# Expert stages: logits of all groups added into one bank, statistics two groups ahead, lists in tile pairs, scatters ahead of later gathers

## The chip, the cores and the metric

The kernel runs as one launch on one core of one Trainium2 chip. The metric is the device time in microseconds. Of the kernel before there are three timed runs and one profiled execution. The core has a matrix engine (PE, with its weight loads as PEld), a vector engine (DVE), an activation engine (ACT), a general engine (POOL) that also issues gathers and scatters by index, and SP, which issues plain transfers.

## What is computed

Three layers follow each other on x, 8192 tokens of 256 numbers in fp32: a mixture of experts, attention, and the same mixture of experts again.

```python
x = x + 0.5 * ffn(layernorm(x))
x = x + attn(layernorm(x))
x = x + 0.5 * ffn(layernorm(x))
```

Only the two ffn layers matter here. Their routing, cut to its core:

```python
probs = softmax(xf @ gate_w.T)            # 8192 tokens, 8 experts
order = argsort(-probs)                   # experts of a token, likeliest first
# a token chooses experts until their probabilities reach 0.9
# an expert keeps 1024 tokens at most: those with the highest p - rank
scores = where(chosen & kept, probs, 0)
h = gelu(xf @ w1[e].T); y = h @ w2[e].T   # for each expert e
out = sum over e of scores[:, e] * y
```

## The kernel before

build_ffn is called for each ffn layer (names "ffn1" and "ffn2", shown as ffn). Token p * 64 + t lies on partition p, tile t. An expert stage has these parts.

- **Front.** 16 groups of 4 tiles. SP loads a group into one of four buffers xin (L232). DVE takes mean and variance (statistics, L420 to L427), ACT the root (L351), DVE the reciprocal and the shift (scale, L434 and L435), ACT normalises four tiles (normalise, L356), PE turns the group (turn, L611), ACT copies it out (turn, L364), and PE multiplies it with the gate (logits, L620): 8 rows of 512 logits in one of two banks. DVE copies these into logitT (take_logits, L440). SP writes the normalised rows of groups 0 to 7 to the DRAM table at once, those of 8 to 15 after the last logits (L235).
- **Hand-over.** Eight transfers bring logitT (one expert a partition) into prob (one token block a partition), four from SP and four from ACT (L247, L376). DVE takes the maximum and subtracts it, ACT takes the exponential, DVE compares the experts with each other and PE sums (L469 to L482, L634, L636).
- **Search.** 27 steps of halving find each expert's threshold (L506 to L512, L640).
- **Lists.** For expert e, DVE builds 0/1 matrices that say which slot each token goes to (picks and finish_picks, L558 to L565, in the memory of logitT). PE multiplies them tile by tile, 64 matmuls (slots, L657). DVE takes the list of tokens (take_idx, L545), SP moves it to idx_all (L265).
- **Expert loop.** POOL gathers 1024 rows of the table in 8 instructions (gather, L316). PE turns weights and rows, multiplies with w1 and w2 (L673 to L705), ACT copies and takes Gelu, DVE scales each of 8 tiles of y by slot_score (L573, L578), and POOL adds them to the output in DRAM (scatter, L326).

Each engine works through its own list in order, so what waits holds back all behind it. gather(e) waits until the rows of e - 2 are turned, its slot_score is taken and list e is there; scatter(e) waits for all of y of e and for the landing of scatter(e - 1). POOL's order is written out:

```python
for e in range(NE):
    if e + 2 < NE:
        gather(e + 2)
    scatter(e)
```

PE's order is slots(0), slots(1), then expert(e), slots(e + 2). DVE's is picks(e + 2), finish_picks(e + 2), expert(e), take_idx(e + 2).

## Time and profile before

| | us |
|---|---|
| median of three runs | 3117.75 (3116.11 to 3124.43) |
| profiled execution, its own time | 3118.9 |
| its span | 3117.1 |
| expert stages | 431 and 431 |
| attention | 2255 |

| engine | busy us | share |
|---|---|---|
| PE | 2613.3 | 84% |
| PEld | 2049.8 | 66% |
| DVE | 1689.6 | 54% |
| ACT | 1684.7 | 54% |
| POOL | 537.1 | 17% |

The profile is one execution. Its times run from the start of the span. Shares are means over stages with different limits, so each stage is read by itself: in the timeline a row has its start, its duration, the engine, the line and operation, what it writes from what, how often, and in brackets how long its engine stood idle before it and what ended that. The granted clock is a share of TensorE's full 2.4 GHz; at 0.5 it is 1.2 GHz.

### The profile page before, as it was taken

What the parts mean: (1) busy time and instruction counts of PE and PEld (TensorE: products, weight loads), DVE (VectorE), ACT (ScalarE), POOL (GpSimd) and SP (SyncE); (2) the same over time, 40 slices, a digit from 0 to 9 for tenths busy, and PEclk for the clock granted to TensorE, in tenths of its full rate; (3) what the DMA queues carried; (4) which work ended last, traced back from release to release, by engine and by line L of the source; (5) the groups of instructions that cost most, each with busy time, mean ns of one, the idle gap of its engine ahead of it and who ended that gap; (6) DMA issues with size and microseconds to landing.
All of it is one profiled execution on the core that took longest, in us unless ns stands there. A gap on an engine that the chain in (4) does not pass through costs nothing. (4 is left out here: it accounts for less than half of the span.)

```text
span 3117.1 us, 106343 instructions
## 1 busy us (share of the span) xinstructions
PE 2613.3 (84%) x48002; PEld 2049.8 (66%) x48004; DVE 1689.6 (54%) x3557; ACT 1684.7 (54%) x2130; POOL 537.1 (17%) x527
## 2 busy tenths in 40 slices
PE   6369924554999999999999999999999999562995
PEld 2157712223888888888888788888898888322674
DVE  5543218887667666665766576656322222356331
ACT  5112203334777777777777777777666666330221
POOL 1028740000100000010001000000000000100586
PEclk8668966666999999999999999999999999885887
DMA  5615531001111111112111211121111111541465
GB/s 162 178 43 101 95 51 31 27 28 48 39 56 49 39 56 45 55 44 67 52 52 49 62 53 52 44 67 43 56 41 47 41 47 34 155 115 26 87 103 67
DMA packets 172434, 195.31 MB, mean 63 GB/s; under 512 B 35600, under 2 KB 151328, under 8 KB 171808
## 3 DMA queue, kind: packets, MB, share of 16 engines
q1 hardware_dynamic: 145056, 153.27, 16.6%
q0 software_dynamic: 24576, 34.10, 7.0%
q8 instruction: 407, 6.67, 0.9%
q10 hardware_dynamic: 2304, 0.53, 0.2%
q14 instruction: 91, 0.75, 0.1%
HBM read 119.10 MB, written 76.02 MB: 63 GB/s over the span
## 5 line engine op out<-in xcount | busy, mean ns | idle before, releaser
L1090 ACT ACTIVATE at_ew<-at_ring 128x1024 f32<-128x1024 f32 (+2 forms) x1280 | 1116.8, 899 | 402.6 <-PE at_ring L1465 287.5
L1488 PEld LDWEIGHTS at_mix<-at_val,at_ew 128*64 128x64 f32 x34816 | 1212.5, 137 | 155.1 <-issue 20.7
L1488 PE MATMUL at_mix<-at_val,at_ew 128*64 128x68 f32 x34816 | 1259.2, 223 | 4.5 <-issue 3.9
L1465 PE MATMUL at_ring<-at_qT,at_kT 98*64 98x512 bf16 (+3 forms) x5120 | 732.9, 350 | 17.4 <-DMA at_kT<-k_parts 11.6
L1337 DVE TENSOR_TENSOR at_mixed<-at_mix,at_prob 128x272 f32<-128x272 f32 x256 | 112.5, 439 | 572.9 <-PE at_mix L1488 556.2
L1465 PEld LDWEIGHTS at_ring<-at_qT,at_kT 98*64 98x64 bf16 x5120 | 268.0, 111 | 81.5 <-issue 26.4
L1035 POOL TENSOR_TENSOR at_val<-at_prob,at_eps_t 128x64 f32<-128x64 f32 x64 | 19.5, 305 | 1228.2 <-PE at_mix L1488 1228.2
L391 ACT ACTIVATE ffn_w1T<-ffn_pair 128x512 f32<-128x512 f32 x16 | 9.6, 597 | 394.8 <-PE ffn_pair L677 394.8
L1540 PE MATMUL at_side<-at_w_all,at_turned 128*64 128x512 f32 (+1 forms) x1024 | 208.4, 554 | 14.8 <-ACT at_vo L1110 7.8
L326 POOL DMA_INDIRECT out_dram<-ffn_xn,ffn_idx_all x128 | 207.9, 1624 | 47.8 <-issue 37.5
L1469 PE MATMUL at_ring<-at_late_kq,at_ident_b 128*64 128x128 bf16 x2048 | 205.6, 220 | 0.0
L316 POOL DMA_INDIRECT ffn_xn<-table,ffn_idx_all x128 | 128.5, 1004 | 442.5 <-DMA ffn_idx_all<-ffn_idx_hi 384.3
L1340 DVE TENSOR_REDUCE at_summed<-at_mixed 128x68 f32<-128x272 f32 x256 | 160.5, 627 | 8.8
L1540 PEld LDWEIGHTS at_side<-at_w_all,at_turned 128*64 128x64 f32 x1024 | 73.2, 149 | 115.1 <-issue 72.4
L1278 DVE TENSOR_REDUCE at_sums<-at_prods 128x1024 f32<-128x4096 f32 x32 | 141.3, 4416 | 0.3
L657 PE MATMUL ffn_bank<-ffn_logitT 128*32 128x64 bf16 x1024 | 119.0, 290 | 22.5 <-DVE ffn_logitT L565 22.5
L578 DVE TENSOR_SCALAR ffn_xn<-ffn_bank,ffn_slot_score 128x256 f32<-128x256 f32 x128 | 61.7, 484 | 138.7 <-PE ffn_bank L705 138.6
L657 PEld LDWEIGHTS ffn_bank<-ffn_logitT 128*32 128x32 bf16 x1024 | 114.8, 137 | 27.2 <-DVE ffn_logitT L565 23.2
L1038 POOL TENSOR_TENSOR at_val<-at_vo,at_val 128x1024 f32<-128x1024 f32 x64 | 130.0, 2032 | 5.0
L1469 PEld LDWEIGHTS at_ring<-at_late_kq,at_ident_b 128*64 128x64 bf16 x2048 | 124.5, 111 | 2.8 <-issue 0.3
L1051 POOL TENSOR_TENSOR at_acc<-at_acc,at_prob 128x64 f32<-128x64 f32 x28 | 8.9, 319 | 664.8 <-PE at_side L1587 664.8
L705 PE MATMUL ffn_bank<-ffn_w2T,ffn_xn 128*128 128x256 f32 x512 | 116.6, 384 | 3.1 <-DVE ffn_xn L578 3.1
(222 smaller groups left out, 3016.3 us busy)
## 6 DMA issues: line engine op xcount, KB each, us to landing
table<-ffn_xn SPq DMA_DIRECT2D x32, 512.0 KB, 6.1
q_parts<-at_parts SPq DMA_DIRECT2D x64, 192.0 KB, 2.4
k_parts<-at_parts SPq DMA_DIRECT2D x64, 192.0 KB, 2.8
at_qT<-q_parts SPq DMA_DIRECT2D x64, 192.0 KB
at_kT<-k_parts SPq DMA_DIRECT2D x64, 192.0 KB
ffn_xin<-in_L_attn_x_dram SPq DMA_DIRECT2D x16, 512.0 KB, 4.2
ffn_w_in<-in_L_ffn_w_dram SPq DMA_DIRECT2D x32, 256.0 KB, 3.3
at_xin<-out_dram SPq DMA_DIRECT2D x32, 256.0 KB, 3.4
```

Of the source, the lines that this page charges most:

```text
L316: pool.indirect_dma_start(out=rows[e % 2][:, j, :], out_offset=None, in_=table, in_offset=bass.IndirectOffsetOnAxis(ap=idx_all[:, e * J + ...
L326: pool.indirect_dma_start(out=dst, out_offset=bass.IndirectOffsetOnAxis(ap=idx_all[:, e * J + j:e * J + j + 1], axis=0), in_=y[e % 2][:, j ...
L657: last = pe.matmul(idx_ps_bank[0:SLOT_HI, 0:2 * SLOT_LO], pick_hi[q][:, :, t], pick_lo[q][:, :, t], start=(t == 0), stop=(t == T - 1))
L705: last = pe.matmul(bank[2 + j % 2][:, 0:D], hT[:, f, j * P:(j + 1) * P], w2T[q][:, f, :], start=(f == 0), stop=(f == FK - 1))
L1038: pool.tensor_tensor(val[q][:, :, :, 0:HD], vv.unsqueeze(2).to_broadcast([P, TB, K, HD]), val[q][:, :, :, HD].unsqueeze(3).to_broadcast([P ...
L1090: act.activation(ew[u % NE_BUF][:, 0:w], ring[u % 2][:, 0:w], ACT.Exp).then_inc(s["exp_ready"], 1)
L1278: ch(dve.tensor_reduce(sums[:, :, :].rearrange("p c n -> p (c n)"), prods[:, :, :].rearrange("p c (n k) -> p (c n) k", k=K), AX.X, ALU.add))
L1340: ch(dve.tensor_reduce(summed[:, :, :], mixed[:, :, :, :].rearrange("p t k w -> p t w k"), AX.X, ALU.add))
L1465: lastm = pe.matmul(ring[u % 2][h:h + HALF, at:at + w], kT[q][:, (j + n) * P + h:(j + n) * P + h + HALF], qT[q][:, c * 512 + t * P:(c + 1) ...
L1469: lastm = pe.matmul(ring[u % 2][h:h + HALF, at:at + P], ident_b[:, h:h + HALF], late_kq[:, :], start=False, stop=True)
L1488: lastm = pe.matmul(mix[c % 2][h:h + HALF, t * K * VW:(t + 1) * K * VW], ew[u % NE_BUF][:, col + h:col + h + HALF], val[q][:, j + n, :, :] ...
L1540: lastm = pe.matmul(side[h:h + HALF, g * 512:g * 512 + n], turned[0][:, g * DK + k, h:h + HALF], w_all[:, k, first:first + n], start=(k == ...
```

## The change

It touches build_ffn alone, in seven places.

1. The gate lies in gateZ, 8 columns of weights between two blocks of 120 columns of zeros. For group g a window of 128 columns is taken so that the 8 gate columns write rows 8g to 8g + 7. All 32 logit matmuls add into bank[0]. ACT copies the bank once, PE turns it in four pieces into bank[1], and DVE reads it there. The 16 copies and the 8 transfers of logits go.
2. DVE runs the statistics two groups ahead of scale (three sets of buffers), with six xin buffers. It normalises the first of four tiles itself, ACT the other three.
3. SP stores groups 0 to 5 in the front and 6 to 15 after the last group.
4. digits, pick_hi and pick_lo keep two tiles beside each other: index (t // 2, digit, t % 2) in place of (digit, t).
5. POOL scatters e before it gathers e + 2, and waits for each tile of y by itself.
6. DVE takes slot_score of e before it builds list e + 2, and waits for the landing of scatter(e - 2) only after that.
7. ACT loads the table of Gelu during routing.

```diff
-    XB = 4
-    EARLY = G // 2
+    XB = 6
+    SB = 3
+    EARLY = 6
+    ZW = P - NE
...
-        gateT = sb("gateT", [P, DK, NE])
-
-        xin = [sb(f"xin{b}", [P, GT, D]) for b in range(XB)]
+        gateZ = sb("gateZ", [P, DK, ZW + NE + ZW])
+
+        front = sb("front", [P, XB * GT * D + 2 * DK * GT * P])
...
+        def pairs(tile, at, n):
+            return tile[:, at:at + n].bitcast(BF16).rearrange("p (t d i) -> p t d i", t=T // 2, i=2)
+
+        PK = SLOT_LO * T // 2
+        pick_hi = [pairs(front, 3 * q * PK, PK) for q in range(2)]
+        pick_lo = [pairs(front, 3 * q * PK + PK, 2 * PK) for q in range(2)]
+        pick_p = [a[:, :, 0:SLOT_LO, :] for a in pick_lo]
+        pick_t = [a[:, :, SLOT_LO:, :] for a in pick_lo]
...
-                    sp.wait_ge(xn_ready, g + 1)
+                    sp.wait_ge(xn_act, g + 1)
+                    sp.wait_ge(xn_dve, g + 1)
                     if g + XB < G:
                         load(g + XB)
                     if g < EARLY:
                         store(g)
-                sp.wait_ge(logits_ready, G)
-                for e in range(1, NE, 2):
-                    sp.dma_start(prob[:, e, :], logitT[e:e + 1, :].rearrange("e (p t) -> e p t", t=T)).then_inc(logits_moved, 16)
                 for g in range(EARLY, G):
                     store(g)
                 sp.wait_ge(order_ready, 1)
...
                 def scatter(e):
                     if e >= 1:
                         pool.wait_ge(added, e * J * 16)
-                    pool.wait_ge(y_ready, e * J + J)
                     for j in range(J):
+                        pool.wait_ge(y_ready, e * J + j + 1)
...
                 for e in range(NE):
+                    scatter(e)
                     if e + 2 < NE:
                         gather(e + 2)
-                    scatter(e)
...
-                act.wait_ge(logits_ready, G)
-                for e in range(0, NE, 2):
-                    act.dma_start(prob[:, e, :], logitT[e:e + 1, :].rearrange("e (p t) -> e p t", t=T)).then_inc(logits_moved, 16)
+                act.wait_ge(logits_ps, G)
+                act.activation(logitG[:, :], bank[0][:, :], ACT.Copy).then_inc(logits_ready, 1)
...
+                    if g >= SB:
+                        dve.wait_ge(xn_act, g - SB + 1)
...
-                dve.wait_ge(consts_ready, 2)
+                    dve.tensor_scalar(xnG[g][:, 0, :], xin[g % XB][:, 0, :], mv[q][:, 0, 0:1], rstd[q][:, 0:1],
+                                      ALU.subtract, ALU.mult).then_inc(xn_dve, 1)
+
+                for g in range(2):
+                    statistics(g)
                 for g in range(G):
-                    if g + 1 < G:
-                        statistics(g + 1)
+                    if g + 2 < G:
+                        statistics(g + 2)
                     scale(g)
-                    if g >= 2:
-                        take_logits(g - 2)
-                take_logits(G - 2)
-                take_logits(G - 1)
...
-                dve.wait_ge(logits_moved, MOVES)
-                ch(dve.tensor_reduce(row_t[:, :], by_t(prob), AX.X, ALU.max))
-                dve.tensor_tensor(work[:, :, :], prob[:, :, :], over_e(row_t[:, :]), ALU.subtract).then_inc(shifted, 1)
+                row_g = row_t[:, :].rearrange("p (g t) -> p g t", t=GT)
+                logit = bank[1][:, :].rearrange("p (t g e) -> p t g e", t=GT, g=G)
+                dve.wait_ge(turns_ps, G + 2)
+                ch(dve.tensor_reduce(row_g, logit.rearrange("p t g e -> p g t e"), AX.X, ALU.max))
+                dve.tensor_tensor(work[:, :, :].rearrange("p e (g t) -> p e g t", t=GT),
+                                  logit.rearrange("p t g e -> p e g t"),
+                                  row_g.unsqueeze(1).to_broadcast([P, NE, G, GT]), ALU.subtract).then_inc(shifted, 1)
...
+                shape = [P, T // 2, SLOT_LO, 2]
...
                     def of(a):
-                        return a[:, e, :].unsqueeze(1).to_broadcast(shape)
-
-                    ch.add(dve.tensor_tensor(pick_hi[q], digits[:, :, :], of(hi), ALU.is_equal))
-                    ch(dve.tensor_tensor(pick_lo[q][:, 0:SLOT_LO, :], digits[:, :, :], of(lo), ALU.is_equal))
-                    ch(dve.tensor_tensor(pick_lo[q][:, SLOT_LO:, :], pick_lo[q][:, 0:SLOT_LO, :],
-                                         count_b[:, :].unsqueeze(1).to_broadcast(shape), ALU.mult))
+                        return a.rearrange("p (t i) -> p t i", i=2).unsqueeze(2).to_broadcast(shape)
+
+                    digit = digits[:, :, :].unsqueeze(1).to_broadcast(shape)
+                    ch.add(dve.tensor_tensor(pick_hi[q], digit, of(hi[:, e, :]), ALU.is_equal))
+                    ch(dve.tensor_tensor(pick_p[q], digit, of(lo[:, e, :]), ALU.is_equal))
+                    ch(dve.tensor_tensor(pick_t[q], pick_p[q], of(count_b[:, :]), ALU.mult))
 
                 def finish_picks(e):
                     q = e % 2
-                    dve.tensor_scalar(pick_lo[q][:, 0:SLOT_LO, :], pick_lo[q][:, 0:SLOT_LO, :], part[:, 0:1], None,
-                                      ALU.mult).then_inc(picks_ready, 1)
+                    dve.tensor_scalar(pick_p[q], pick_p[q], part[:, 0:1], None, ALU.mult).then_inc(picks_ready, 1)
 
                 def expert(e):
                     q = e % 2
                     dve.wait_ge(gathered[q], (e // 2 + 1) * 16 * J)
+                    dve.tensor_scalar(slot_score[q][:, :], rows[q][:, :, D + e], 0.5, None, ALU.mult
+                                      ).then_inc(slot_score_ready, 1)
+                    if e + 2 < NE:
+                        picks(e + 2)
+                        finish_picks(e + 2)
+                    dve.wait_ge(slot_score_ready, e + 1)
                     if e >= 2:
                         dve.wait_ge(added, (e - 1) * J * 16)
-                    dve.tensor_scalar(slot_score[q][:, :], rows[q][:, :, D + e], 0.5, None, ALU.mult
-                                      ).then_inc(slot_score_ready, 1)
-                    dve.wait_ge(slot_score_ready, e + 1)
...
                 def logits(g):
                     pe.wait_ge(xnT_ready, g + 1)
-                    if g >= 2:
-                        pe.wait_ge(logits_ready, g - 1)
+                    at = ZW - g * NE
                     for k in range(DK):
-                        last = pe.matmul(bank[g % 2][0:NE, :], gateT[:, k, :], xnT[g % 2][:, k, :],
-                                         start=(k == 0), stop=(k == DK - 1))
+                        last = pe.matmul(bank[0][:, :], gateZ[:, k, at:at + P], xnT[g % 2][:, k, :],
+                                         start=(g == 0 and k == 0), stop=(g == G - 1 and k == DK - 1))
                     last.then_inc(logits_ps, 1)
 
...
                 logits(G - 1)
+                pe.wait_ge(logits_ready, 1)
+                for t in range(GT):
+                    last = pe.transpose(bank[1][:, t * P:(t + 1) * P], logitG[:, t * P:(t + 1) * P], ident[:, :])
+                last.then_inc(turns_ps, 1)
...
-                        last = pe.matmul(idx_ps_bank[0:SLOT_HI, 0:2 * SLOT_LO], pick_hi[q][:, :, t], pick_lo[q][:, :, t],
-                                         start=(t == 0), stop=(t == T - 1))
+                        last = pe.matmul(idx_ps_bank[0:SLOT_HI, 0:2 * SLOT_LO], pick_hi[q][:, t // 2, :, t % 2],
+                                         pick_lo[q][:, t // 2, :, t % 2], start=(t == 0), stop=(t == T - 1))
```

POOL, from its last constants to the end of the expert stage (L316 and L318 gather, L326 and L328 scatter). Before:

```order
L305 MEMSET ffn_restart 128x8
L306 COPY ffn_digits<-ffn_count_b 128x2048
L316 DMA ffn_xn<-table,ffn_idx_all 128x264 x24
L326 DMA out_dram<-ffn_xn,ffn_idx_all 8192x256 x8
L316 DMA ffn_xn<-table,ffn_idx_all 128x264 x8
...
L326 DMA out_dram<-ffn_xn,ffn_idx_all 8192x256 x24
```

The same place in the changed kernel:

```order
L307 MEMSET ffn_restart 128x8
L308 COPY ffn_digits<-ffn_count_b 128x64
L318 DMA ffn_xn<-table,ffn_idx_all 128x264 x16
L328 DMA out_dram<-ffn_xn,ffn_idx_all 8192x256 x8
L318 DMA ffn_xn<-table,ffn_idx_all 128x264 x8
...
L328 DMA out_dram<-ffn_xn,ffn_idx_all 8192x256 x16
```

Two batches of gathers and not three stand ahead of the first scatters, and two batches of scatters and not three are left at the end.

DVE, one group in the steady front (ffn_mv and ffn_var are mean and variance). Before:

```order
L435 SCALAR_TENSOR_TENSOR ffn_shift<-ffn_mv,ffn_rstd 128x4
L440 COPY ffn_logitT<-ffn_bank 8x4x128
L420 BN_STATS ffn_stats<-ffn_xin 128x6 x4
L423 BN_AGGR ffn_mv<-ffn_stats 128x2 x4
L427 TENSOR_SCALAR ffn_var<-ffn_mv 128x4
L434 RECIPROCAL ffn_rstd<-ffn_std 128x4
```

The same place in the changed kernel (ffn_front holds xin):

```order
L434 SCALAR_TENSOR_TENSOR ffn_shift<-ffn_mv,ffn_rstd 128x4
L436 TENSOR_SCALAR ffn_xn<-ffn_front,ffn_mv,ffn_rstd 128x256
L421 BN_STATS ffn_stats<-ffn_front 128x6 x4
L426 BN_AGGR ffn_mv<-ffn_stats 128x2 x4
L428 TENSOR_SCALAR ffn_var<-ffn_mv 128x4
L433 RECIPROCAL ffn_rstd<-ffn_std 128x4
```

The copy that waits for PE's logits is gone; a normalisation of one tile, which waits for nothing of PE, stands there.

## Rows read from the trace of the kernel before

**Rows 1.** busy us by stage: PE, PEld, DVE, ACT, POOL; then clock, DMA share, GB/s

```profile
0.00:431.00 431.00, 281.07 (x1337) 189.41 (x1338) 176.23 (x498) 100.18 (x167) 177.99 (x151) 0.78 0.50 110
...
2686.00:3117.00 431.00, 282.93 (x1337) 190.03 (x1338) 176.27 (x498) 98.89 (x166) 177.62 (x147) 0.75 0.44 91
```

**Rows 2.** the timeline, steady front: start, us, engine, line, operation, [idle before, its end]

```profile
52.07 1.10 PE L611 MATMUL ffn_pair<-ffn_ident,ffn_xn 128*128 128x128 f32 x8
...
52.18 1.04 DVE L440 COPY ffn_logitT<-ffn_bank 8x512 f32<-8x512 f32 x1 [3.70 <-PE ffn_bank L620]
...
53.10 1.88 PE L620 MATMUL ffn_bank<-ffn_xnT,ffn_gateT 128*8 128x512 f32 x4
...
55.38 2.07 ACT L356 ACTIVATE ffn_xn<-ffn_xin,ffn_shift,ffn_rstd 128x256 f32<-128x256 f32 x4
...
57.36 1.00 ACT L364 ACTIVATE ffn_xnT<-ffn_pair 128x1024 f32<-128x1024 f32 x1
...
57.50 1.09 PE L611 MATMUL ffn_pair<-ffn_ident,ffn_xn 128*128 128x128 f32 x8 [2.52 <-ACT ffn_xn L356]
...
62.01 1.09 PE L611 MATMUL ffn_pair<-ffn_ident,ffn_xn 128*128 128x128 f32 x8
```

**Rows 3.** the table of busy time, a stretch of the front, one around the second list

```profile
16.00:50.00 34.00, 26.02 (x90) 11.63 (x91) 20.27 (x84) 23.36 (x48) 0.00 (x0) 0.87 0.74 222
...
182.00:205.00 23.00, 16.18 (x133) 15.33 (x131) 8.48 (x12) 1.09 (x2) 10.28 (x9) 0.50 0.25 71
```

**Rows 4.** the timeline, start of the front

```profile
13.90 1.40 DVE L420 BATCH_NORM_STATS2 ffn_stats<-ffn_xin 128x6 f32<-128x256 f32 x4
...
16.11 1.40 DVE L420 BATCH_NORM_STATS2 ffn_stats<-ffn_xin 128x6 f32<-128x256 f32 x4
...
16.24 1.94 PE L611 MATMUL ffn_pair<-ffn_ident,ffn_xn 128*128 128x128 f32 x8 [13.33 <-ACT ffn_xn L356]
```

**Rows 5.** the timeline, from the front to routing

```profile
95.41 13.05 SPq L235 DMA_DIRECT2D table<-ffn_xn  x8
...
101.99 1.01 DVE L459 TENSOR_REDUCE ffn_row_t<-ffn_prob 128x64 f32<-128x512 f32 x1 [12.81 <-DMA ffn_prob<-ffn_logitT]
...
121.58 2.58 SPq L252 DMA_DIRECT2D ffn_key<-ffn_order  x4
```

**Rows 6.** the timeline, end of the search, first list, first gather

```profile
171.09 0.19 PE L644 MATMUL ffn_bank<-ffn_total,ffn_before 128*128 128x8 bf16 x1 [3.96 <-DVE ffn_total L522]
...
171.19 0.17 PE L647 MATMUL ffn_bank<-ffn_total,ffn_ones 128*128 128x8 bf16 x1
...
181.42 7.43 PE L657 MATMUL ffn_bank<-ffn_logitT 128*32 128x64 bf16 x64 [10.06 <-DVE ffn_logitT L565]
...
183.67 1.23 DVE L560 TENSOR_TENSOR ffn_logitT<-ffn_logitT,ffn_count_b 128x2048 bf16<-128x2048 bf16 x1
...
192.14 1.19 POOL L316 DMA_INDIRECT ffn_xn<-table,ffn_idx_all  x1 [180.48 <-DMA ffn_idx_all<-ffn_idx_hi]
```

**Rows 7.** the timeline, expert loop: DVE, POOL and PE

```profile
216.84 0.48 DVE L578 TENSOR_SCALAR ffn_xn<-ffn_bank,ffn_slot_score 128x256 f32<-128x256 f32 x1 [11.19 <-PE ffn_bank L705]
...
233.35 1.86 POOL L316 DMA_INDIRECT ffn_xn<-table,ffn_idx_all  x1 [19.75 <-PE ffn_pair L685]
...
248.66 7.44 PE L657 MATMUL ffn_bank<-ffn_logitT 128*32 128x64 bf16 x64
...
257.40 2.82 POOL L326 DMA_INDIRECT out_dram<-ffn_xn,ffn_idx_all  x1 [0.31 <-issue]
...
275.00 7.43 PE L657 MATMUL ffn_bank<-ffn_logitT 128*32 128x64 bf16 x64
...
365.70 1.02 POOL L316 DMA_INDIRECT ffn_xn<-table,ffn_idx_all  x1 [1.65 <-DMA ffn_idx_all<-ffn_idx_hi]
...
410.00 1.55 POOL L326 DMA_INDIRECT out_dram<-ffn_xn,ffn_idx_all  x1 [2.53 <-DMA out_dram<-ffn_xn,ffn_idx_all]
...
423.00 1.55 POOL L326 DMA_INDIRECT out_dram<-ffn_xn,ffn_idx_all  x1 [0.30 <-issue]
```

More of the change, by code:

```diff
@@ L97, in build_ffn @@
         gate_in = sb("gate_in", [NE, D])
[L98 to L100 removed]
+        gateZ = sb("gateZ", [P, DK, ZW + NE + ZW])
+        front = sb("front", [P, XB * GT * D + 2 * DK * GT * P])
         xn = sb("xn", [P, T * D])
[L102 to L109 removed]
+        stats = [sb(f"stats{q}", [P, GT, 6]) for q in range(SB)]
+        mv = [sb(f"mv{q}", [P, GT, 2]) for q in range(SB)]
+        var = [sb(f"var{q}", [P, GT]) for q in range(SB)]
+        std = [sb(f"std{q}", [P, GT]) for q in range(SB)]
+        rstd = [sb(f"rstd{q}", [P, GT]) for q in range(SB)]
+        shift = [sb(f"shift{q}", [P, GT]) for q in range(SB)]
+        logitG = sb("logitG", [P, GT * P])
         prob = sb("prob", [P, NE, T])
@@ L132, in build_ffn, with words @@
         lo = sb("lo", [P, NE, T], mybir.dt.int16)
-        def words(tile, at, n, shape, dt=F32):
-            flat = tile[:, at:at + n]
-            if dt != F32:
-                flat = flat.bitcast(dt)
-            return flat.rearrange("p (a b) -> p a b", a=shape[0])
-        PH, PL = SLOT_LO * T // 2, SLOT_LO * T
-        pick_hi = [words(logitT, q * PH, PH, (SLOT_LO, T), BF16) for q in range(2)]
-        pick_lo = [words(logitT, 2 * PH + q * PL, PL, (2 * SLOT_LO, T), BF16) for q in range(2)]
-        xnG = [words(xn, g * GT * D, GT * D, (GT, D)) for g in range(G)]
-        rows = [words(xn, q * J * ROW, J * ROW, (J, ROW)) for q in range(2)]
+        def words(tile, at, n, rows):
+            return tile[:, at:at + n].rearrange("p (a b) -> p a b", a=rows)
+        def pairs(tile, at, n):
[5 more added lines that the diff above has]
+        pick_t = [a[:, :, SLOT_LO:, :] for a in pick_lo]
+        xin = [words(front, b * GT * D, GT * D, GT) for b in range(XB)]
+        xnT = [words(front, XB * GT * D + q * DK * GT * P, DK * GT * P, DK) for q in range(2)]
+        xnG = [words(xn, g * GT * D, GT * D, GT) for g in range(G)]
+        rows = [words(xn, q * J * ROW, J * ROW, J) for q in range(2)]
         used = 2 * J * ROW
-        y = [words(xn, used + q * J * D, J * D, (J, D)) for q in range(2)]
+        y = [words(xn, used + q * J * D, J * D, J) for q in range(2)]
         used += 2 * J * D
-        xeT = words(xn, used, DK * CAP, (DK, CAP))
-        hT = words(xn, used + DK * CAP, FK * CAP, (FK, CAP))
+        xeT = words(xn, used, DK * CAP, DK)
+        hT = words(xn, used + DK * CAP, FK * CAP, FK)
         tile_of = sb("tile_of", [SLOT_HI, SLOT_LO])
@@ L344, in _ @@
             def _(act):
[L345 to L346 removed]
+                act.wait_ge(turns_ps, 1)
+                act.activation(gateZ[:, :, ZW:ZW + NE], bank[1][:, 0:DK * NE].rearrange("p (k e) -> p k e", k=DK),
                                ACT.Copy).then_inc(gateT_ready, 1)
@@ L350, in root @@
                     act.wait_ge(var_ready, g + 1)
-                    act.activation(std[g % 2][:, :], var[g % 2][:, :], ACT.Sqrt).then_inc(std_ready, 1)
+                    act.activation(std[g % SB][:, :], var[g % SB][:, :], ACT.Sqrt).then_inc(std_ready, 1)
                 def normalise(g):
                     act.wait_ge(rstd_ready, g + 1)
-                    for t in range(GT):
+                    for t in range(1, GT):
                         last = act.activation(xnG[g][:, t, :], xin[g % XB][:, t, :], ACT.Identity,
-                                              bias=shift[g % 2][:, t:t + 1], scale=rstd[g % 2][:, t:t + 1])
-                    last.then_inc(xn_ready, 1)
+                                              bias=shift[g % SB][:, t:t + 1], scale=rstd[g % SB][:, t:t + 1])
+                    last.then_inc(xn_act, 1)
                 def turn(g):
-                    act.wait_ge(xnT_ps, g + 1)
+                    act.wait_ge(turns_ps, g + 2)
                     if g >= 2:
                         act.wait_ge(logits_ps, g - 1)
-                    act.activation(xnT[g % 2][:, :, :], pair[g % 2][:, :, :], ACT.Copy).then_inc(xnT_ready, 1)
+                    act.activation(xnT[g % 2], pair[g % 2][:, :, :], ACT.Copy).then_inc(xnT_ready, 1)
                 root(0)
@@ L379, in _ @@
                 act.activation(prob[:, :, :], work[:, :, :], ACT.Exp).then_inc(exped, 1)
+                act.activation(std[1][:, :], var[1][:, :], ACT.Gelu)
                 act.wait_ge(order_ready, 1)
```

61 lines of the change are left out of this document (19 added, 42 removed).

## The prediction, made before the changed kernel ran

> **What bounds the kernel now.** I read the busy time by stage first. It cuts the run into an expert stage of 431 us, attention, and a second expert stage of 431 us whose counts and busy times are those of the first within 2 us [rows 1]. The change touches the expert stages alone, so I work out one, with its times, and take it twice. Attention (2686 - 431 = 2255 us) stays.
>
> In an expert stage four stretches follow each other: the front (layer norm and logits, 16 groups), the hand-over to routing, the search and lists, and the expert loop. The timeline of each shows which wait ends last.
>
> *Front.* Two turns of PE, the second ones of two pairs of groups, start at 52.07 and 62.01: 9.94 us for two groups, 4.97 each. The reader is to see a ring in it. DVE stands 3.70 us before a copy of logits because the copy of group g-2 is queued ahead of the statistics of the next group; so ACT gets its variance late, and PE its rows 2.52 us late [rows 2]. No engine is full. PE is busy 26.02 of 34 us, at a mean granted clock of 0.87: it changes between 2.4 GHz, where a turn takes 1.10 us, and 1.2 GHz, where one takes 1.94 [rows 2 to 4].
>
> *Hand-over.* From the last logits to the first reduction DVE waits 12.81 us for transfers of logitT to prob [rows 5].
>
> *Search and lists.* The 27 search steps are not touched. Then 64 small matmuls per expert list take 7.43 us, 116 ns a pair of weight load and matmul [rows 6].
>
> *Loop.* Two engines are full here. PE repeats every 26.3 us (248.66 to 275.00). POOL repeats every 26.2 us: gathers begin at 233.35 and, five batches later, at 365.70, less 1.35 of an idle 1.65. Of it 8 scatters at 1.86 (1.55 and 0.30 idle, as at 423.00) are 14.9, and some 1.3 are lost where DVE builds a list (the scatter at 257.40 takes 2.82 and not 1.55); that leaves 10.0 for 8 gathers. But POOL stood idle 19.75 us before 233.35, although outputs of expert 0 were there from 217.3 on: gather(2) was in front of scatter(0). At the other end three batches of scatters are left. The last begins at 410.00, 2.53 us after the one before, whose landing it waits for, and its last instruction starts at 423.00 [rows 7].
>
> **The change part by part, one expert stage.**
>
> *Front: logits added in one bank, statistics two ahead, one normalisation of four on DVE.* The logit copies and their waits go; the ring is open. Next late is the fullest engine. PE: a turn 1.03 (52.07 to 53.10) and logits 1.88, 2.9 us a group; the gate now has 128 columns, the rows streamed are still 512, so I add nothing. ACT: three normalisations of 0.52, a turn of 1.00 and a root of 0.2, 2.75. DVE: 2.21 a group now (13.90 to 16.11) and at most 0.48 more for 256 elements, the price of L578, 2.7 [rows 2, 4, 7]. The hand-offs fit: ACT's turn of g-1 runs beside PE's turn of g. One wait is new: DVE's aggregates for g+2 wait until ACT has normalised g-1, and scale(g) is queued behind them. From there to the shift are 0.8 us of DVE work (2.21 less 1.40), during which ACT has its turn of 1.00 to do; it costs ACT some 0.1. So 2.9 us a group at 2.4 GHz. From below 2.7 (DVE or ACT); from above 4.97 as today.
>
> The start gains nothing: POOL's constants hold DVE as now, and three groups of statistics come before the first scale. PE starts at 15.8 (16.24 less one normalisation) and at the low clock, a turn 1.94. With two low turns and one set of logits the third turn starts at 22.6 (estimate). Thirteen groups later, at 60.3, comes turn 15; then 1.05 of turn, twice 1.85 of logits, 0.65 for ACT's copy of the bank (512 elements, an estimate from 1.00 for 1024), 0.6 for four transposes, 0.1: the reduction starts at 66.4 where it started at 101.99. **Saved: 35.6 us**, of which 12.8 is the transfer wait. The reduction and subtraction now read PSUM with strides: between -0.4 and +0.5 us, taken as 0.
>
> The stores: ten and not eight follow the last group. They were issued in 13.05 us for eight, 1.63 each; 16.3 us from 60.2 to 76.5, landed by about 82. The keys are moved at 66.4 + 19.6 = 86 (121.58 - 101.99 = 19.6) [rows 5]. So they keep clear, by some 4 us; if not, the keys wait for the difference. The Gelu table load moves beside DVE's compares; it stood beside running matmuls, so 0.
>
> *Lists in tile pairs.* Before, neighbouring elements of an operand of the list matmuls lay 64 elements (128 bytes) apart, now 2 (4 bytes). At 190 us the granted clock is 0.50, in the loop it is mostly high, and lists take 7.43 or 7.44 us in both [rows 3, 6, 7], so what limits is not the array's clock. Nearest row without a stride: the four matmuls of 8 columns with 128-column weights, the first of which starts at 171.09 and the last at 171.19, 33 ns apart. So a list costs between 64 x 33 ns = 2.1 and 7.4 us. I take 3.9 at the high clock and 4.5 at the low one, nearer the row without stride but with 64 columns to stream. The Trainium skill (SBUF - State Buffer, the note on cachelines) has SBUF lines of 16 bytes, full rate with two or more hits a line, and a penalty on each new line: 8 bf16 may be strided for free. By that rule the old lists pay on every element and the new ones nothing; the trace's equal time at two clocks agrees with it, and it would put the lists at the low end, which saves at most 1 us more a stage.
>
> The first list is followed by DVE's second one, which ends at 184.90 (183.67 + 1.23), before take_idx; so at most 4.0 us are won. **Saved before the first gather: 2.9 us** (0 to 4.0).
>
> *Scatters ahead of later gathers; DVE takes slot_score before the next list.* Time from the first gather on (192.14 before). Gather 0 is free of DVE's list 2, which now waits for it: landed at 12.0 (13.3 before); the first output comes 11.8 us after landing (DVE stood 11.19 between its slot_score and that output [rows 7], and the two take 0.65). So scatter 0 starts at 24.0, in what was idle. Then seven batches of scatters and six of gathers follow without a gap, 26.2 a pair: scatter 6 starts at 24.0 + 157.2 = 181.2, ends at 196.1, scatter 7 waits 2.5 us for that landing, as the batch at 410.00, starts at 198.6; its last instruction at 211.6. Before: 423.00 - 192.14 = 230.9. What is behind the new wait: gather(e+2) stands behind scatter(e), which waits for y of e; PE has expert e+1 to do meanwhile. PE needs 26.3 - 3.5 = 22.8 a period, so it has 3.4 us to spare, and y of 7 is there some 4 us before scatter 7. POOL is the only bound. **Saved: 19 us**, 18.6 with a hand-off (from 0 if PE starves to 20).
>
> **Sum.** 35.6 + 2.9 + 18.6 = 57.1 us a stage, 114.2 in two. The profiled execution took 3118.9 us (span 3117.1), 1.15 above the median of the three runs, 3117.75. 3118.9 - 114.2 = 3004.7, **forecast 3005 us** (its own range 2990 to 3018: 2.7 us a group gives 6 less, 3.1 six more, the rest from lists and hand-offs).
>
> **Rivals.**
> 1. *The clock stays at 1.2 GHz in the front.* For it: the mean is 0.87 now, and the start is low [rows 3, 4]. Against: the fall follows gaps of 2.5 us and more, which go. A group takes 1.94 + 3.5 = 5.4 us (twice 1.88 is 3.8, less what overlaps); the reduction comes at about 107, 5 us later than now. A stage still saves 16: 3087. Chance 0.05.
> 2. *The new list layout halves DVE's rate.* Three of the four list operations take 1.23 for 2048 bf16 elements; with one operand in runs of two they could take 2.4. Then the first index comes 3.2 us later and not 2.9 earlier, and POOL loses one more us at each of six lists: 13 us a stage, 3030. The Trainium skill (VectorE: DVE Perf Modes, what auto-detection checks) asks of 16-bit operands only a step of one innermost, which the pair layout keeps; that speaks against this rival. Chance 0.08.
> 3. *List matmuls do not get faster.* Then PE's period stays 26.3, its first output of expert 7 comes at 24 + 7 x 26.3 = 208.1, 9.5 us behind 198.6, and the 2.9 are lost: 12.4 us a stage, 3030. Against: equal time at two clocks. Chance 0.09.
> 4. *The reordering brings nothing*, since gathers come late and PE starves: 3005 + 37 = 3042. Against: PE's spare time above. Chance 0.04.
> 5. *Slower: list matmuls get slower*, because both operands now hit the same lines of memory. A list of L us gives PE a period of 18.9 + L; scatter 7 then ends at 24 + 7 (18.9 + L) + 14.9 = 171.2 + 7L after the first gather, against 232.8 now, and the first gather comes L - 7.4 later. The 35.6 us of the front are eaten where 8L - 69 exceeds them, from L = 13.1, 204 ns a pair against 116. At 256 ns, L = 16.4, a stage is 26.6 us longer: 3172. No row speaks for it. Chance 0.02.
>
> **How the numbers follow.** The forecast has 0.71, the rivals 0.28, and 0.01 is left for sums that cancel. The range reaches from the forecast's low end to rivals 2, 3 and partly 4: 2988 to 3040. A measurement tells 0.3%, some 9 us, from no change. Faster 0.97, same 0.01, slower 0.02.
>
> **What would show it.** Front: PE turns about 2.9 us apart with the clock at 1.0; no DVE wait before a logit copy; the reduction near 66. If ACT or DVE is full and PE waits, the 2.9 was wrong. Lists: L657's successor under 4 us. Loop: a scatter batch near 24 us after the first gather, 26.2 us per pair on POOL, no idle time over 0.5 us but before scatter 7; PE waiting for gathers. A first expert stage longer than 380 us would make the forecast wrong.

## The result, and the profile after

The changed kernel takes 3007.3 us (median of 4 runs, 3003.83 to 3009.3) beside 3118.22 us of the kernel before on the same chip (3116.11 to 3124.43): ratio 0.964, interval 0.9623 to 0.9657. The forecast was 3005. The profiled execution took 3003.83 us, its span is 3002.0.

The windows of the two expert stages, with the columns of [rows 1], and of the front stretch of 34 us that [rows 3] has:

```profile
0.00:378.70 378.70, 239.74 (x1342) 158.47 (x1342) 165.15 (x498) 92.27 (x153) 182.72 (x152) 0.82 0.53 125
2630.70:3002.00 371.30, 238.64 (x1342) 159.57 (x1342) 164.81 (x498) 91.17 (x152) 181.00 (x148) 0.80 0.48 105
16.00:50.00 34.00, 33.40 (x150) 20.66 (x150) 29.77 (x149) 33.58 (x66) 0.00 (x0) 1.00 0.72 245
```

The first expert stage ends 52.5 us earlier (378.73, not 431.27), the second takes 371.3 us instead of 431, and attention between them is 2.7 us shorter. In the front PE is busy for 33.40 of 34 us and ACT for 33.58; the granted clock is 1.00 (2.4 GHz) where its mean was 0.87.

*Front.* The timeline of its steady part, against [rows 2]:

```profile
25.84 1.58 ACT L357 ACTIVATE ffn_xn<-ffn_front,ffn_shift,ffn_rstd 128x256 f32<-128x256 f32 x3
26.23 1.04 PE L608 MATMUL ffn_pair<-ffn_ident,ffn_xn 128*128 128x128 f32 x8
27.10 1.88 PE L616 MATMUL ffn_bank<-ffn_front,ffn_gateZ 128*128 128x512 f32 x4
27.33 1.00 ACT L365 ACTIVATE ffn_front<-ffn_pair 128x1024 f32<-128x1024 f32 x1
28.23 0.19 ACT L352 ACTIVATE ffn_std<-ffn_var 128x4 f32<-128x4 f32 x1
28.42 1.59 ACT L357 ACTIVATE ffn_xn<-ffn_front,ffn_shift,ffn_rstd 128x256 f32<-128x256 f32 x3
28.82 1.04 PE L608 MATMUL ffn_pair<-ffn_ident,ffn_xn 128*128 128x128 f32 x8
```

Turns are 2.59 us apart, where they were 4.97. No row has a wait. The reader is to see that starts lie closer than durations allow: the logits begin 0.87 us after the turn, not its 1.04.

*Hand-over and first list*, DVE and PE, against [rows 5, 6]:

```profile
60.60 0.69 DVE L453 TENSOR_REDUCE ffn_row_t<-ffn_bank 128x64 f32<-128x512 f32 x1 [10.71 <-PE ffn_bank L627]
```

```profile
139.76 3.52 PE L657 MATMUL ffn_bank<-ffn_front 128*32 128x64 bf16 x64 [10.06 <-DVE ffn_front L562]
...
144.49 2.06 PE L657 MATMUL ffn_bank<-ffn_front 128*32 128x64 bf16 x64 [1.21 <-DVE ffn_front L562]
```

The reduction comes at 60.60, 41.4 us earlier than at 101.99. These two lists take 3.52 us (granted clock 0.53) and 2.06 us (1.00), where a list took 7.43 or 7.44 at 0.50 and at 0.69 to 0.86. DVE's list operations stay at 1.22, 1.22, 1.23 and 0.75.

In the loop only the list of expert 2 looks so (2.07 us at 182.29). Those of experts 3 to 7 take 8.1 to 8.9 us from their first matmul to their last, and 7.3 to 8.3 in the second stage. Here is that of expert 4, PE, with the DVE row that takes it:

```profile
229.12 1.27 PE L657 MATMUL ffn_bank<-ffn_front 128*32 128x64 bf16 x37
230.90 0.29 PE L657 MATMUL ffn_bank<-ffn_front 128*32 128x64 bf16 x4 [0.50 <-issue]
232.32 0.28 PE L657 MATMUL ffn_bank<-ffn_front 128*32 128x64 bf16 x4 [1.14 <-issue]
...
237.33 0.39 PE L657 MATMUL ffn_bank<-ffn_front 128*32 128x64 bf16 x4 [0.29 <-issue]
...
239.73 0.18 DVE L542 COPY ffn_tile_of<-ffn_bank 32x32 f32<-32x32 f32 x1 [10.02 <-remote]
```

37 pairs run at full pace, the others in groups of one to five with pauses of up to 1.2 us, for which the rows name nothing that PE waited for. From 200 to 330 us these pauses make 24.1 us, and PE's other waits 1.1. With its pauses PE is full there, with a period of 27.5 us.

*Loop*, POOL and ACT, against [rows 7]:

```profile
158.08 0.95 POOL L318 DMA_INDIRECT ffn_xn<-table,ffn_idx_all  x1 [0.30 <-issue]
...
177.56 1.64 POOL L328 DMA_INDIRECT out_dram<-ffn_xn,ffn_idx_all  x1 [10.81 <-DVE ffn_xn L577]
...
185.11 3.77 POOL L328 DMA_INDIRECT out_dram<-ffn_xn,ffn_idx_all  x1 [0.30 <-issue]
189.18 1.74 POOL L328 DMA_INDIRECT out_dram<-ffn_xn,ffn_idx_all  x1 [0.30 <-issue]
...
194.95 1.02 POOL L318 DMA_INDIRECT ffn_xn<-table,ffn_idx_all  x1 [0.30 <-issue]
...
222.42 1.02 POOL L318 DMA_INDIRECT ffn_xn<-table,ffn_idx_all  x1 [0.30 <-issue]
```

```profile
160.39 1.02 ACT L399 ACTIVATE ffn_xn<-ffn_pair 128x1024 f32<-128x1024 f32 x1 [11.69 <-PE ffn_pair L685]
165.63 1.02 ACT L399 ACTIVATE ffn_xn<-ffn_pair 128x1024 f32<-128x1024 f32 x1 [4.22 <-remote]
169.14 1.08 ACT L407 ACTIVATE ffn_xn<-ffn_bank 128x512 f32<-128x512 f32 x2 [2.48 <-remote]
```

The first gather is at 146.54, the first scatter 31.0 us behind it (forecast 24.0), and POOL's pair of batches takes 27.5 us (194.95 to 222.42; forecast 26.2). Its last instruction starts 223.9 us after the first gather in the first stage and 218.8 in the second, where before it was 230.9 and 231.1: 7.0 and 12.2 us saved, not 18.6. Two things stand in these rows. ACT copies the second half of expert 0's turned rows at 165.63, although PE's turns (started 158.38, 3.68 long) are over at 162.06; the row names no engine of the core for that wait of 4.22, nor for the 2.48 after it. And where DVE's list starts with a scatter (185.10 and 185.11) that scatter takes 3.77 us and the next 1.74, where 1.55 is usual: 2.4 lost a list, not 1.3. POOL has no idle time over 0.31 us in the pairs, so POOL and PE both fill 27.5 us.

### The profile page after: what moved, and what is told of

It is laid out like the page before. It is cut to its first block and busy times, and to the rows that moved or that the text cites. A ratio compares the mean times of both kernels' runs of the same rounds, so it can differ in the third digit from the quotient of the medians.

```text
span 3002.0 us, 106279 instructions
## 1 busy us (share of the span) xinstructions
PE 2526.9 (84%) x48012; PEld 1984.4 (66%) x48012; DVE 1667.9 (56%) x3557; ACT 1669.4 (56%) x2102; POOL 545.4 (18%) x529
## 5 line engine op out<-in xcount | busy, mean ns | idle before, releaser
L1035 POOL TENSOR_TENSOR at_val<-at_prob,at_eps_t 128x64 f32<-128x64 f32 x64 | 19.6, 306 | 1228.2 <-PE at_mix L1488 1228.2
L328 POOL DMA_INDIRECT out_dram<-ffn_xn,ffn_idx_all x128 | 223.1, 1743 | 60.8 <-issue 36.0
L318 POOL DMA_INDIRECT ffn_xn<-table,ffn_idx_all x128 | 123.6, 965 | 308.8 <-DMA ffn_idx_all<-ffn_idx_hi 270.4
L697 PE MATMUL ffn_bank<-ffn_xn,ffn_w1T 128*128 128x512 f32 x256 | 119.4, 620 | 8.2 <-issue 4.6
L705 PEld LDWEIGHTS ffn_bank<-ffn_w2T,ffn_xn 128*128 128x128 f32 x512 | 90.6, 189 | 30.4 <-issue 17.7
```

Source lines behind the costliest of these rows:

```text
L318: pool.indirect_dma_start(out=rows[e % 2][:, j, :], out_offset=None, in_=table, in_offset=bass.IndirectOffsetOnAxis(ap=idx_all[:, e * J + ...
L328: pool.indirect_dma_start(out=dst, out_offset=bass.IndirectOffsetOnAxis(ap=idx_all[:, e * J + j:e * J + j + 1], axis=0), in_=y[e % 2][:, j ...
L697: last = pe.matmul(bank[n % 2][:, :], w1T[q][:, k, f * P:(f + 1) * P], xeT[:, k, s * 512:(s + 1) * 512], start=(k == 0), stop=(k == DK - 1))
L705: last = pe.matmul(bank[2 + j % 2][:, 0:D], hT[:, f, j * P:(j + 1) * P], w2T[q][:, f, :], start=(f == 0), stop=(f == FK - 1))
```

## Experiments

Unless it says otherwise each is one edit of the changed kernel, timed in three rounds beside the kernel before, whose median in the three groups was 3122.3 (a to d), 3123.85 (e to h) and 3115.84 (i to l). Each group ran on another chip, so times of different groups are compared by their ratio to it; the changed kernel's is 0.964.

**a. The loop put back.**

```
 for e in range(NE):
-    scatter(e)
     if e + 2 < NE:
         gather(e + 2)
+    scatter(e)
     # scatter waits for all J outputs; picks(e + 2) first, as before
```

> The changed kernel with the expert loop alone put back: POOL issues gather(e+2) ahead of scatter(e), a scatter batch waits for all eight outputs, and DVE builds list e+2 ahead of slot_score(e). Front and lists in tile pairs stay. Theory 1 (what the loop is worth is what its two profiles show: 7.0 us in the first stage and 12.2 in the second): 3007 + 19 = 3026 us, and POOL's last scatter starts 231 us after its first gather. Theory 2 (the reordering is worth the forecast 18.6 a stage, and what was lost came from the other parts of the change): 3007 + 37 = 3044. By theory 1 ACT's gap of 4.22 us between the two copies of expert 0 is gone with the reordering; by theory 2 it is still there.

Measured: 3021.59 us, ratio 0.9674 (0.9657 to 0.969). POOL's last instruction starts 231.6 and 229.9 us after the first gather. So as it runs, the reordering is worth 19.3 us by the two profiled spans (3021.3 and 3002.0) but 0.0034 or 10.6 us by the ratios; both are far from theory 2's 37. ACT's gap between its two copies is down to 1.22 us, but it still has gaps in expert 0 (3.60 us before its second Gelu; 2.46 and 2.22 in the second stage), so theory 1 had their cause wrong: the reordering doesn't make them.

**b. The old list layout.**

```
-shape = [P, T // 2, SLOT_LO, 2]
+shape = [P, SLOT_LO, T]
-pick_hi[q][:, t // 2, :, t % 2]
+pick_hi[q][:, :, t]
```

> The changed kernel with the operands of the list matmuls back in the old layout (digit, then tile). Theory 1 (PE is not the bound of the loop, since POOL needs 27.5 us a pair): only the first list is paid, 3.9 us a stage, 3007 + 8 = 3015 us; list matmuls take 7.43, POOL's pair stays at 27.5, the operations of DVE at 1.22. Theory 2 (PE bounds the loop at 26.3 us and more, as rival 3 of the prediction had it): 12.4 us a stage, 3032, with POOL idle before scatter batches.

Measured: 3016.6 us, ratio 0.9663 (0.9647 to 0.9679). The first gather is 3.8 us later (150.37), the last scatter starts 221.1 and 224.2 us behind it. ACT has gaps here too (2.48 and 1.53 us, 4.66 and 1.80 in the second stage). The time is theory 1's, but POOL's rows are theory 2's: the loop does wait for PE, before nearly every gather.

```profile
276.01 1.02 POOL L318 DMA_INDIRECT ffn_xn<-table,ffn_idx_all  x1 [2.15 <-PE ffn_pair L685]
```

Five such waits in the first stage take 1.4 to 2.2 us each, and pairs take 26.4 to 27.8. The last batch of scatters starts 208.1 and 211.2 us after the first gather, and 208.1 is what rival 3 had worked out for old lists. In the changed kernel, whose pairs take 27.5 for another reason, it starts at 210.9 and 205.8, in l at 200.2 and 198.4.

**c. The front alone.** Edits a and b together.

> Loop and lists both put back, so that only the front of the change is left. Theory 1 (the front is worth the 41.4 us that the two profiles differ by at the first reduction): 3118 - 83 = 3035 us. Theory 2 (part of it is given back at the stores, the keys or the first gather): 3118 - 71 = 3047, what the prediction had credited to the front (35.6 a stage). If the parts add, c is after + what a_old_loop and b_old_lists lose.

Measured: 3041.65 us, ratio 0.9743 (0.9727 to 0.9759), 80.6 us less than before, 40.3 a stage. The first gather is at 150.88, 41.3 us earlier than before, so nothing is lost up to there. The loop then takes 4 us more than before (last instruction 234.9 us after the first gather, against 230.9). POOL waits 1.3 to 3.2 us before gathers, for PE's lists or the turns behind them. ACT has no gap here, although gather(1) runs beside it. By the ratios, a loses 0.0034, b 0.0023 and both together 0.0103: the parts don't add. The waits in b and c suggest why: old lists bound the loop once nothing else does. No run takes this apart further.

**d. No early table load.**

```
-act.activation(std[1][:, :], var[1][:, :], ACT.Gelu)
```

> The changed kernel without the early Gelu on one small tile that loads the table; the table is then loaded at the first real Gelu (1.28 us). Theory 1 (ACT's stall in expert 0, 4.22 and 2.48 us in the first stage, has to do with that instruction or with where it moves ACT's later instructions in its code): the stall goes, some 6 us less a stage in the first and 4 in the second, 2998 us with the table load paid. Theory 2 (ACT is held back there by POOL's gathers of expert 1, whatever its code): the stall stays and 1.3 us a stage are added, 3010.

Measured: 3005.34 us, ratio 0.9633 (0.9617 to 0.9649), no different from the changed kernel. The gap before the second copy is 4.97 and 5.07 us; the table load lies inside the second wait. Theory 1 fell as far as this instruction goes. The loop shows something else. The first scatter is as late as in the changed kernel (31.1 us after the first gather), yet the four pairs with a list take 25.7 to 26.0 us in the first stage, and two of 25.8 and two of 27.6 in the second. In the pair that ends at 221.15 DVE's list starts at 213.17, 0.12 us behind the start of a scatter, and the next one takes 2.04 and not 3.8:

```profile
213.05 1.55 POOL L328 DMA_INDIRECT out_dram<-ffn_xn,ffn_idx_all  x1 [0.30 <-issue]
214.91 2.04 POOL L328 DMA_INDIRECT out_dram<-ffn_xn,ffn_idx_all  x1 [0.30 <-issue]
```

In the changed kernel, at 212.58, it starts 0.03 us ahead of the scatter, which then takes 3.75.

**e. The list spread over the outputs.**

```
 for j in range(J):
     ... y[q][:, j, :] ...
+    if e + 2 < NE:
+        pick_step(e + 2, j)   # one of the four operations for j = 0 to 3
```

> The changed kernel with the four operations of list e+2 spread over DVE's outputs of expert e: one behind each of the first four outputs, instead of all in a row behind slot_score(e). Theory 1 (what POOL loses is one wait for a whole row of list operations of DVE, 2.4 us a list because a scatter starts together with the row): with gaps between them, and beside gathers, the pair of POOL shrinks from 27.5 towards 25.15, what the pair without a list takes; at 25.5, 12 us a stage, 2985 us. Theory 2 (POOL loses per operation of DVE, however they lie): the pair stays at 27.5 and the time at 3007. If PE starves for the later list, POOL shows idle time before scatter batches.

Measured: 2997.15 us, ratio 0.9589 (0.9568 to 0.961). Pairs take 26.6 us (247.65 to 274.20): between the theories. Of each list three gathers are still slow, taking 1.6 to 1.7, 1.19 and 1.58 us instead of 0.95. ACT's gaps stay (first scatter 31.2 us after the first gather), and PE still pauses within its lists from expert 4 on (5.3 to 5.4 us).

**f. The list behind the outputs.**

```
 for j in range(J):
     ... y[q][:, j, :] ...
+if e + 2 < NE:
+    picks(e + 2)
+    finish_picks(e + 2)
```

> The changed kernel with list e+2 built in one row behind DVE's eight outputs of expert e, beside POOL's gathers and not in the middle of a scatter batch. Theory 1 (it depends on where in POOL's instructions the row starts): the loss per list is that seen beside gathers, 0.2 to 1.4 us, pairs of 25.4 to 26.6 and 2984 to 2998 us. Theory 2 (place does not matter): 27.5 and 3007. A side cost is possible, PE waiting 4.4 us for the list of e+2, since it has some 5 us to spare a pair.

Measured: 3027.63 us, ratio 0.969 (0.9673 to 0.9707), slower than the changed kernel. The side cost that I had called possible decides: PE waits for the list, and POOL for PE.

```profile
248.21 3.60 PE L657 MATMUL ffn_bank<-ffn_front 128*32 128x64 bf16 x64 [4.89 <-DVE ffn_front L562]
```

```profile
254.88 1.02 POOL L318 DMA_INDIRECT ffn_xn<-table,ffn_idx_all  x1 [4.22 <-PE ffn_pair L685]
```

**g. No lists for experts 2 to 7.** DVE's `picks` and `finish_picks` are left out there, and PE uses the old operands.

> Leaves out part of the computation: the lists of experts 2 to 7 are not built by DVE, PE runs their matmuls on the operands left by experts 0 and 1. It prices DVE's lists to POOL. Theory 1 (the whole difference between pairs of 27.5 and 25.15 us is DVE's list operations holding POOL back): all pairs take 25.15, 14 us a stage less, 2979 us. Theory 2 (PE, or the landing of scatters, bounds the pair close behind): pairs stay above 26 with POOL idle between batches, over 2990 us.

Measured: 2984.08 us, ratio 0.9554 (0.9536 to 0.9572). The beginnings of gather batches 3 and 4:

```profile
192.85 1.02 POOL L318 DMA_INDIRECT ffn_xn<-table,ffn_idx_all  x1 [0.30 <-issue]
...
217.96 1.02 POOL L318 DMA_INDIRECT ffn_xn<-table,ffn_idx_all  x1 [0.30 <-issue]
```

All pairs take 25.1 us: what stands between 25.1 and 27.5 is DVE's lists. This is shown. PE still pauses within its lists here (lists of 4.8 to 8.6 us), so the pauses alone do not hold POOL at 27.5.

**h. gather(1) held back** until ACT has copied expert 0's rows.

```
 gather(0)
+pool.wait_ge(turned, 3)
 gather(1)
```

> The changed kernel with gather(1) held back until ACT has copied all of expert 0's turned rows (three increments of its semaphore), in the 10.8 us for which POOL stood idle before scatter 0. Theory 1 (ACT's gaps of 4.22 and 2.48 us in expert 0 come from the gather that runs beside them): the gaps go, the first scatter starts 24 us after the first gather instead of 31.0 and 27.4, and the time is 2997 us. Theory 2 (they have another cause): the gaps stay and the time is 3007 or more, since gather(1) may now end after the first output.

Measured: 2991.74 us, ratio 0.9577 (0.9558 to 0.9596). ACT's gaps are gone:

```profile
160.16 1.02 ACT L400 ACTIVATE ffn_xn<-ffn_pair 128x1024 f32<-128x1024 f32 x1 [11.65 <-PE ffn_pair L686]
161.87 1.02 ACT L400 ACTIVATE ffn_xn<-ffn_pair 128x1024 f32<-128x1024 f32 x1 [0.68 <-PE ffn_pair L686]
164.39 0.60 ACT L408 ACTIVATE ffn_xn<-ffn_bank 128x512 f32<-128x512 f32 x1 [1.50 <-PE ffn_bank L698]
```

The first scatter starts at 173.16, 26.8 us after the first gather, right behind the held gather(1). And pairs take 26.6 us in this stage, without a change to the lists: the loop starts at another time, and the lists fall elsewhere in scatter batches (1.5 lost in the sixth scatter and the next). PE's pauses stay (lists of 7.0 to 9.0 us).

**i. Edits h and e together.**

> h_gather1_late and e_spread together. Theory 1 (the two act on different things: the hold takes away ACT's gaps in expert 0, the spreading what POOL loses to lists): their gains add, 15.6 + 10.2 us below the changed kernel's 3007.3, 2982 us. Theory 2 (part of the gain of h_gather1_late was that the start moved and DVE's list fell on another place of a scatter, pairs of 26.2 to 26.6 instead of 27.5; spread lists have pairs of 26.6 too): no more than h alone, 2990 to 2993 us, pairs of 26.6.

Measured: 2989.96 us, ratio 0.9599 (0.9583 to 0.9615); profiled, 2987.7 against 2991.6 of h, but h's ratio is 0.9577: not told apart. Theory 2: the gains don't add. Pairs take 25.9 to 26.6, and PE's lists 2.07 us throughout.

**j. Edit h, and the list in one row behind the first output of e.**

> h_gather1_late, and list e+2 built in one row behind DVE's first output of expert e, where POOL is at its gathers. Theory 1 (a row beside gathers costs 0.2 to 1.4 us): pairs of 25.4 to 26.5 and 2980 to 2990 us. Theory 2 (the other seven outputs wait 4.4 us for the row, PE's outputs with them, and POOL runs dry as it did in f_late): POOL idle before gathers, 3000 us and more.

Measured: 2990.79 us, ratio 0.9599 (0.9583 to 0.9615). Pairs take 26.1 us (241.29 to 267.39), POOL doesn't run dry in them, and the row costs what theory 1 gave it beside gathers: the sixth gather takes 2.0 us instead of 0.95. PE's lists take 2.07 us. Not told apart from h or i.

**k. Half of the logits left out.**

```
-for k in range(DK):
+for k in range(1):
     last = pe.matmul(bank[0][:, :], gateZ[:, k, at:at + P], ...)
```

> Leaves out part of the computation: the logits of a group take only the first of their two 128-row halves of the contraction, which frees PE of 0.9 us a group. It asks what sets the 2.59 us between PE's turns in the front. Theory 1 (ACT and DVE, each without idle time at 2.59): turns stay 2.59 apart, the first reduction comes about 1 us earlier for the last group alone, 3005 us. Theory 2 (PE, as the prediction had it): turns come down to 1.9 to 2.4 apart, 0.2 to 0.7 x 14 groups less a stage, 2987 to 3001 us. The clock may fall if PE stands idle; then turns take 1.94 and the time goes up.

Measured: 2978.87 us, ratio 0.9564. PE in the front:

```profile
27.44 1.09 PE L608 MATMUL ffn_pair<-ffn_ident,ffn_xn 128*128 128x128 f32 x8 [0.55 <-ACT ffn_xn L357]
30.02 1.09 PE L608 MATMUL ffn_pair<-ffn_ident,ffn_xn 128*128 128x128 f32 x8 [0.55 <-ACT ffn_xn L357]
```

Turns stay 2.58 us apart with PE idle for 0.55: PE does not set the pace, theory 1. ACT is busy for 33.58 of the 34 us and DVE for 29.75, neither with a wait in the rows, and no run tells which of the two sets it. The reduction came 2.95 us earlier (57.65), not 1. The rest of the gain was a surprise: ACT's gaps in expert 0 are gone (first scatter 25.5 us after the first gather), with ACT's code unchanged, and one matmul fewer a group in PE's. PE's pauses are gone too: every list in the loop takes 2.07 us.

**l. ACT's loop code moved by 40 instructions.**

```
 act.activation(std[1][:, :], var[1][:, :], ACT.Gelu)
+for n in range(40):
+    act.activation(padding[:, n, :], var[1][:, :], ACT.Gelu)
```

> The changed kernel with 40 more small activations (128x4) on ACT behind its table load, in time in which ACT waits for the keys: they only move the instructions of the expert loop further on in ACT's code. Theory 1 (ACT's gaps in expert 0 are waits for its own instructions to be fetched, and depend on where in the code they stand): the gaps of 4.22 and 2.48 us and of 3.56 and 1.81 us change by over 2 us or go. Theory 2 (they come from gather(1) issued by POOL at the same time, whatever ACT's code): they stay within 1 us, first scatters 31 and 27 us after the first gathers, 3007 us.

Measured: 2986.32 us, ratio 0.9585 (0.9569 to 0.9601), the shortest time here with the whole computation (by ratio not told apart from h, i and j), and faster than the changed kernel (0.9623 to 0.9657), with 40 needless instructions more.

```profile
160.17 1.02 ACT L402 ACTIVATE ffn_xn<-ffn_pair 128x1024 f32<-128x1024 f32 x1 [11.67 <-PE ffn_pair L688]
161.88 1.02 ACT L402 ACTIVATE ffn_xn<-ffn_pair 128x1024 f32<-128x1024 f32 x1 [0.68 <-PE ffn_pair L688]
```

```profile
171.84 1.65 POOL L329 DMA_INDIRECT out_dram<-ffn_xn,ffn_idx_all  x1 [5.34 <-DVE ffn_xn L580]
...
188.91 1.02 POOL L319 DMA_INDIRECT ffn_xn<-table,ffn_idx_all  x1 [0.30 <-issue]
...
199.01 1.61 POOL L329 DMA_INDIRECT out_dram<-ffn_xn,ffn_idx_all  x1 [0.30 <-issue]
200.93 2.42 POOL L329 DMA_INDIRECT out_dram<-ffn_xn,ffn_idx_all  x1 [0.30 <-DVE ffn_slot_score L570]
203.65 2.06 POOL L329 DMA_INDIRECT out_dram<-ffn_xn,ffn_idx_all  x1 [0.30 <-issue]
```

The gaps are gone with gather(1) in its old place. The first scatter is 25.5 us behind the first gather, a list costs POOL 1.4 us (2.42 and 2.06 for 1.55 each), pairs take 25.1 to 26.4, and the last instruction of the two stages starts 213.3 and 211.4 us after the first gather. The forecast's 211.6 was the loop without the gap. PE's pauses are gone as well. Its lists take 2.07 us, and it waits for gathers, as the forecast had it:

```profile
217.03 2.07 PE L660 MATMUL ffn_bank<-ffn_front 128*32 128x64 bf16 x64
...
226.95 3.68 PE L688 MATMUL ffn_pair<-ffn_ident,ffn_xn 128*128 128x128 f32 x16 [6.82 <-DMA ffn_xn<-table,ffn_idx_all]
```

## Why the prediction was right, step by step

The time was right within 2.3 us, in part because errors cancelled. The sum said 114.2 us; the profiled executions differ by 115.1.

1. *Front, 35.6 us: too little.* It saved 41.4. The ring did open, by the cause named, and the clock rose. The term mis-sized was 2.9 us a group; it is 2.59, below even the 2.7 given as the lowest, and over thirteen groups that is 4.0 us. The third turn started at 21.04, not 22.6, which is 1.6 more (PE started at 14.17, not 15.8). I added durations of neighbours on one engine (1.03 and 1.88; 2.75 for ACT), but their starts lie closer: on ACT 1.49, 0.90 and 0.19 make 2.58. I named PE as the bound; experiment k shows that it is ACT or DVE. Experiment c shows that the front keeps what it wins: 41.3 at the first gather.
2. *Hand-over and stores: right.* The keys move at 79.85, 19.25 us after the reduction (19.6 forecast), and nothing collides.
3. *Lists, 2.9 us: low by 1 for the first list, and wrong in the loop.* I chose 3.9 and 4.5 us a list between bounds of 2.1 and 7.4; measured are 2.06 and 3.52. The low bound was the truth at the high clock, 32 ns a pair. The Trainium skill (SBUF - State Buffer, the note on cachelines) had it there: the trace agrees, with 116 ns a pair at a stride of 128 bytes at granted clocks of 0.50 to 0.86. DVE's rate was not halved (rival 2). But from expert 3 on PE's list takes 7.3 to 8.9 us with its pauses, about as long as the old 7.44 or longer. So PE did not need 22.8 us a period with 3.4 to spare, as forecast, and POOL was not the only bound: PE filled 27.5. Rival 3 had its condition wrong, since the matmuls do get faster, and its mechanism right: with old lists b starts its last batch of scatters 208.1 us after the first gather (211.2 in the second stage), where it gave 208.1, and POOL waits for PE.
4. *Loop, 18.6 us: the step that failed* as measured, 7.0 and 12.2. Its mechanism was right: in l, where ACT has no gap, it saves 17.6 and 19.6. Two parts were missed. ACT's gaps put off scatter 0 (31.0 and 27.4 us after the first gather; 25.5 and 25.1 in l). Of the 1.5 us that l still has over the forecast's 24.0, 1.0 lies between slot_score and the first output (12.4 us, 11.4 before), where PE now starts after 10.8 us of idle time at a granted clock of 0.50 (0.63 before, at 205 to 210). And the 1.3 us that a list costs POOL was taken over from the row of before [rows 7], though it depends on when the list starts within a scatter: 2.4 in the changed kernel, 1.4 in l, 0 in g. What moves DVE's list is what it waits for. In the changed kernel it stands behind take_idx, and so behind PE's late list (DVE's copy at 239.73, its next list at 240.13, a scatter of 3.80 us at 240.10); in l PE's list is early, DVE waits for the landed rows instead (200.58), and its list falls on the second scatter. The late start of the loop alone does not do it: d starts as late and has pairs of 25.7 to 26.0.
5. *The other rivals.* The clock did not stay low (1; its 107 us for the reduction should have been about 104 by its own terms). The reordering brought something (4). The list matmuls did not get slower (5), though some lists as a whole did, to 8.9 us, by pauses that no rival had. Attention, forecast to stay, got 2.7 us shorter; no run says why.

What stays open is what ACT waits for in its gaps. Shown is that they go when gather(1) is moved (h), when ACT has 40 more instructions ahead (l) and when PE has one matmul fewer a group (k), but not with one instruction fewer on ACT (d). Kernel c has neither edit and no gap, while a and b, its two halves, each keep gaps. Open in the same way is why PE pauses within its lists. It does in the changed kernel, a, d, e, g and h, where it has no long wait for another engine or a gather between 200 and 330 us (1.2 us at most), and not in f, i, j, k and l, where it has some (3.6 to 7.7 us). That goes together in all eleven, and is not shown to be the cause. ACT's gaps and PE's pauses come apart in f, which has only the gaps, and in h, which has only the pauses; l has neither, so its gain can't be put down to ACT's gaps alone. Both l and k change more than the place of code: l's new tile also moves what is allocated behind it, and k starts its loop 2.9 us earlier. Neither was tried by itself. A late fetch of instructions behind POOL's descriptors would fit both, but the trace's instruction queues show no packet in ACT's gaps (none between 146 and 182 us), nor in PE's pauses (none between 202 and 226), so it is only argued. Whether l keeps its gain when other code changes was not tried.

## What to carry to other kernels

Where an engine runs without gaps, take the pace from start to start in the trace and not from the sum of durations: here 2.58 us for ACT against a sum of 2.77, and 2.59 for PE against 2.92. A loss by a shared resource is a function of phase, so a price read from one row holds only while the order in time holds; give it bounds from all its rows. A saving measured once, with an engine at rest, need not hold in the loop: look at the same instruction in every place where it runs, as the lists here show. A gap that the rows put down to nothing on the core is worth two cheap experiments, moving the neighbour in time and moving the code.
